# First projection of a two-layer decoder: batches that run into each other, with a second buffer for u and z

## The reference, cut to what matters

```python
x  = h * rsqrt(mean(h**2, -1) + eps) * norm_w            # 256 x 512
xz = x @ in_proj_w.T + in_proj_b                         # 512 -> 2 x 1536
x, z = xz[..., :1536], xz[..., 1536:]
xc = conv over 4 tokens of x, per feature; then u = silu(xc)
z  = silu(z)                                             # the gate
# of u: w_dt @ u and the mean over each of 24 heads (48 numbers a token)
```

## Time and profile before

| | |
|---|---|
| time, median of 3 runs | 4777.92 us (4775.51 to 4779.34) |
| the profiled execution | 4790.36 us, of it span 4788.6 us |
| TensorE / VectorE / ScalarE / GpSimd busy, whole span | 82% / 59% / 35% / 29% |
| mean granted TensorE clock, whole span | 0.914 of full speed |
| first store of u_feat issued (batch 0) | 68.92 us |
| last store of u_feat issued (batch 7) | 429.81 us |
| first instruction of the next stage's queue | 446.71 us |

### The profile page before, as it was taken

How to read it: one execution, slowest core, us unless ns; L and a number is a source line. 1 busy time by engine, 2 the same in 40 slices (tenths; PEclk the granted TensorE clock), 3 DMA queues, 4 the chain that set the end, 5 groups by cost and what they waited for, 6 DMA issues and landing times. The chain is left out here.

```text
span 4788.6 us, 61695 instructions
## 1 busy us (share of the span) xinstructions
PE 3915.2 (82%) x19902; PEld 3042.3 (64%) x19902; DVE 2804.6 (59%) x4963; ACT 1669.4 (35%) x3411; POOL 1386.2 (29%) x1202
## 2 busy tenths in 40 slices
PE   7886899989999597759995994787877689839992
PEld 7886777767777475554445873555556467627772
DVE  5554445454544476972227866999999654533335
ACT  4333322232222120042214764555555422203431
POOL 0000000000000005662225525999999500010002
PEclk9998999999999898969997997999999899959996
DMA  3323433443343452119977544222330211023324
GB/s 110 128 93 126 115 90 86 105 111 91 86 105 91 141 165 69 39 46 336 321 246 220 167 148 162 84 84 84 105 128 29 92 45 66 31 82 103 105 96 119
DMA packets 532330, 556.51 MB, mean 116 GB/s; under 512 B 157795, under 2 KB 431523, under 8 KB 526544
## 3 DMA queue, kind: packets, MB, share of 16 engines
q1 hardware_dynamic: 497728, 470.19, 32.2%
q0 software_dynamic: 29632, 75.97, 4.8%
q10 hardware_dynamic: 4816, 8.53, 0.5%
HBM read 440.09 MB, written 135.43 MB: 120 GB/s over the span
## 5 line engine op out<-in xcount | busy, mean ns | idle before, releaser
L2337 PE MATMUL d_py<-d_h,d_ident 128*128 128x256 f32 x2048 | 522.7, 412 | 177.7 <-POOL d_h L2167 155.4
L2175 POOL TENSOR_TENSOR d_dBu<-d_B,d_dtu 128x1024 f32<-128x1024 f32 x256 | 597.1, 2367 | 118.0 <-DMA d_dt<-dt 118.0
L2337 PEld LDWEIGHTS d_py<-d_h,d_ident 128*128 128x128 f32 x2048 | 412.9, 206 | 284.0 <-POOL d_h L2167 184.3
L723 PE MATMUL a_pB<-a_uhi,a_whi 128*128 128x512 f32 x1152 | 484.6, 421 | 44.2 <-DVE a_ulo L610 44.0
L723 PE MATMUL a_pB<-a_uhi,a_wlo 128*128 128x512 f32 x1152 | 455.8, 396 | 0.0
L723 PE MATMUL a_pB<-a_ulo,a_whi 128*128 128x512 f32 x1152 | 454.5, 395 | 0.0
L2221 ACT ACTIVATE d_ph<-d_dt,d_A 128x255 f32<-128x255 f32 x1024 | 425.8, 461 | 0.1
L2281 DVE TENSOR_TENSOR_SCAN d_ph<-d_ph,d_dBu 128x1024 f32<-128x1024 f32 x160 | 365.9, 2287 | 24.5 <-ACT d_ph L2221 12.1
L1058 POOL TENSOR_TENSOR b_kv<-b_c 128x128 f32 (+11 forms) x256 | 100.3, 431 | 774.1 <-DMA b_c<-ctx_turned 770.4
L530 POOL DMA_DIRECT2D a_uraw<-u_feat x48 | 25.8, 539 | 1023.9 <-DVE a_ulo L610 583.8
L723 PEld LDWEIGHTS a_pB<-a_uhi,a_whi 128*128 128x128 f32 x1152 | 218.8, 190 | 110.6 <-DVE a_wlo L614 36.6
(11 more groups left out here) (481 smaller groups left out, 9384.9 us busy)
## 6 DMA issues: line engine op xcount, KB each, us to landing
c_gu<-w_gu SPq DMA_DIRECT2D x64, 768.0 KB, 6.6
a_wraw<-w_bc SPq DMA_DIRECT2D x48, 768.0 KB, 7.5
a_alall<-alpha SPq DMA_DIRECT2D x24, 1024.0 KB, 5.2
c_wd<-w_down SPq DMA_DIRECT2D x64, 256.0 KB, 7.5
slots_y<-c_y POOLq DMA_DIRECT2D x64, 256.0 KB, 7.1
f_w1r<-w SPq DMA_DIRECT2D x64, 256.0 KB, 2.8
f_w2r<-w SPq DMA_DIRECT2D x64, 256.0 KB, 2.9
d_B<-bc SPq DMA_DIRECT2D x7, 2048.0 KB, 14.2
```

Source lines behind the costliest of these rows:

```text
L723: ins = nc.tensor.matmul(out, a[:, k, cols], b[:, k, ts], start=(k == 0 and n == 0), stop=(k == F - 1 and n == 2))
L2175: pool.tensor_tensor(dBu[c % RB][:, :, :], B_sb[i][:, q * G:(q + 1) * G, :], dtu_sb[i][:, f, :].unsqueeze(1).to_broadcast([P, G, L]), ALU. ...
L2337: ins = nc.tensor.matmul(py[f % 2][:, 0:L], ident_sb[:, :], h_sb[c % RH][:, n, :], start=False, stop=(q == Q - 1 and n == G - 1))
```

## The change: what it does

- u and z get two buffers each. The second ones lie over the 12 raw weight buffers, which are free once batch 0 has split them. xnT_hi and xnT_lo get two buffers each too.
- x of the next batch is turned inside this batch: `stats` in block 5, behind z(4) and u(4); xn on VectorE in block 7; the eight transposes behind pz(8); xnT_hi in block 9, xnT_lo in block 10.
- u's rows are turned in six portions, of 4 blocks and one half of the tokens each. Four stand in the same batch (behind pz(5), pz(6), pz(9), pz(10)), two in the next one (behind pz(1) and pz(2)); each copy by VectorE stands one block later, the last two in blocks 1 and 2 of the next batch.
- dt(0) to dt(10) stand together behind pz(11), since pT serves for turning x before that; dt(11) stands in the next batch behind pz(0). z(11) and u(11) are computed in the next batch behind xpad(0).
- Stores: z_feat ahead of dt_mean. ident and norm_w come by ScalarE's queue with a semaphore of their own, the two weights of dt have another, and TensorE starts when ident and norm_w are there.
- The hardware loop runs three times over two batches.

```diff
-    NORM_AT = 6
+    STATS_AT, NORM_AT, TURN_AT, HI_AT, LO_AT = 5, 7, 8, 9, 10
+    ROWS_AT = {5: 0, 6: 1, 9: 2, 10: 3}
+    KEPT_AT = {6: 0, 7: 1, 10: 2, 11: 3}
...
+        u_sb = [m.sb("u0", [P, F, L]), nc.alloc_sbuf_tensor_at("a1_u1", [P, F, L], F32, offset=over)]
+        z_sb = [m.sb("z0", [P, F, L]), nc.alloc_sbuf_tensor_at("a1_z1", [P, F, L], F32, offset=over + 4 * F * L)]
...
+        def reached(b, done):
+            return max(done, 0) if is_first(b) else b * F + done
+        def rows(n):
+            return n // 2, n % 2
+        def batches(eng, batch):
+            batch(0, 0, False)
+            with eng.Fori(0, NB // 2 - 1) as r:
+                for i in range(2):
+                    batch(2 * r + 1 + i, 1 - i, False)
+            batch(NB - 1, 1, True)
...
 # ScalarE
+            def batch(b, i, last):
+                for f in range(F):
+                    act.wait_ge(s_px, b * F + f + 1)
+                    act.wait_ge(s_conv, reached(b, f - 1))
+                    nc.scalar.activation(xpad[f % 2][:, 3:3 + L], px[f % 2][:, 0:L], ACT.Identity, ...).then_inc(s_xpad, 1)
...
+                    if f >= 1:
+                        gate(b, i, f - 1)
+                        value(b, i, f - 1)
+                    elif not is_first(b):
+                        gate(b - 1, 1 - i, F - 1)
+                        value(b - 1, 1 - i, F - 1)
+                    if f == STATS_AT and not last:
+                        stats(b + 1)
+                    if f == HI_AT and not last:
+                        turned(b + 1, 1 - i)
...
 # VectorE, behind conv(f)
+                    if not is_first(b):
+                        if f == 1:
+                            means(b - 1)
+                            kept(b - 1, 4)
+                        if f == 2:
+                            kept(b - 1, 5)
+                    if f in KEPT_AT:
+                        kept(b, KEPT_AT[f])
+                    if f == NORM_AT and not last:
+                        norm(b + 1, link)
+                    if f == LO_AT and not last:
+                        turned(b + 1, 1 - i)
...
 # TensorE, behind pz(f)
+                    if not is_first(b):
+                        if f == 0:
+                            dt(b - 1, 1 - i, F - 1)
+                        if f == 1:
+                            row_major(b - 1, 1 - i, 4)
+                        if f == 2:
+                            row_major(b - 1, 1 - i, 5)
+                    if f in ROWS_AT:
+                        row_major(b, i, ROWS_AT[f])
+                    if f == TURN_AT:
+                        pe.wait_ge(s_dtm, b)
+                        if not last:
+                            norm(b + 1)
                 if not last:
-                    pe.wait_ge(s_dtm, b + 1)
-                    norm(b + 1)
...
+                    pe.wait_ge(s_xnTl, b * KD + 2 * KD)
+                for k in range(F - 1):
+                    dt(b, i, k)
```

More of the change, by code:

```diff
@@ L123, in group, with is_first @@
                 split(n, *CHUNKS[n])
[L125 to L131, removed]
+        def is_first(b):
+            return isinstance(b, int) and b == 0
+        def reached(b, done):
[8 more added lines that the diff above has]
+            batch(NB - 1, 1, True)
         @block.sync
@@ L144, in load @@
                 sp.dma_start(x_sb[:, :, :], x[bass.ds(b * L, L), :].rearrange("(c p) n -> p c n", p=P)).then_inc(s_x, 16)
-            def batch(b, last, first=False):
+            def batch(b, i, last):
                 if not last:
@@ L187, in stats, with turned @@
                 assert link.count[0] == LINKS_A
-            def turned(b):
+            def turned(b, i):
                 act.wait_ge(s_T, b + 1)
                 for k in range(KD):
-                    nc.scalar.activation(xnT_hi[:, k, :], pT[:, k // 2, (k % 2) * L:(k % 2 + 1) * L], ACT.Copy,
+                    nc.scalar.activation(xnT_hi[i][:, k, :], pT[:, k // 2, (k % 2) * L:(k % 2 + 1) * L], ACT.Copy,
                                          scale=nw_sb[:, k:k + 1]).then_inc(s_xnT, 1)
[L195 to L203, removed]
-                        group(split, f + 2)
-                    if f == NORM_AT and not last:
-                        stats(b + 1)
[L207 to L228, removed]
+            def gate(b, i, g):
+                if g == 0 and not is_first(b):
+                    act.wait_ge(s_out_z, b * 16 - 16)
+                act.wait_ge(s_pz, b * F + g + 1)
+                nc.scalar.activation(z_sb[i][:, g, :], pz[g % 2][:, 0:L], ACT.Silu, bias=bz_sb[:, g:g + 1]).then_inc(s_z, 1)
@@ L230, in _ @@
+            act.wait_ge(s_set, 3)
+            stats(0)
+            group(split, 0)
+            act.wait_ge(s_turner, 32)
+            turned(0, 0)
+            group(split, 1)
+            act.wait_ge(s_const, 64)
+            batches(act, batch)
+            gate(NB - 1, 1, F - 1)
+            value(NB - 1, 1, F - 1)
         @block.vector
@@ L271, in batch @@
                     ins.then_inc(s_conv, 1)
-                    if f == NORM_AT + 1 and not last:
+                    if not is_first(b):
[7 more added lines that the diff above has]
+                    if f == NORM_AT and not last:
                         norm(b + 1, link)
+                    if f == LO_AT and not last:
+                        turned(b + 1, 1 - i)
                 assert last or link.count[0] == LINKS_V
[L275 to L291, removed]
+            norm(0)
+            group(split, 0)
+            dve.wait_ge(s_turner, 32)
+            turned(0, 0)
+            group(split, 1)
+            dve.wait_ge(s_const, 64)
+            batches(dve, batch)
+            means(NB - 1)
+            kept(NB - 1, 4)
+            kept(NB - 1, 5)
         @block.tensor
         def _(pe):
-            pe.wait_ge(s_const, 16 * CONSTS)
+            pe.wait_ge(s_turner, 32)
             def parts(out, a, a_cols, b, b_cols, k):
@@ L310, in norm, with dt @@
                 ins.then_inc(s_T, 1)
-            def batch(b, last, first=False):
-                pe.wait_ge(s_xnTl, b * KD + KD)
[L315 to L321, removed]
+            def dt(b, i, k):
+                if k == 0:
+                    pe.wait_ge(s_heads, 32)
+                pe.wait_ge(s_u, b * F + k + 1)
+                for c in range(2):
+                    ins = nc.tensor.matmul(pT[:, c, 0:H2], u_sb[i][:, k, c * P:(c + 1) * P], wdt_sb[:, k, :], start=(k == 0), stop=(k == F - 1))
+                if k == F - 1:
+                    ins.then_inc(s_dt, 1)
@@ new lines, in row_major, with batch @@
+            def row_major(b, i, n):
+                j, c = rows(n)
+                pe.wait_ge(s_u, b * F + j * 4 + 4)
+                pe.wait_ge(s_ut, max(n - 1, 0) if is_first(b) else b * 6 + n - 1)
+                for q in range(4):
+                    ins = nc.tensor.transpose(pu[n % 2][:, q * P:(q + 1) * P], u_sb[i][:, j * 4 + q, c * P:(c + 1) * P], ident_sb[:, :])
+                ins.then_inc(s_pu, 1)
+            def batch(b, i, last):
+                pe.wait_ge(s_xnTl, b * KD + KD)
+                x_parts = (xnT_hi[i], xnT_lo[i])
```

95 lines of the change are left out of this document (55 added, 40 removed).

## The result

| | before | changed |
|---|---|---|
| time, median | 4777.47 us (4775.51 to 4779.34) | 4731.92 us (4729.30 to 4736.24) |
| profiled execution | 4790.36 us | 4734.08 us |
| last store of u_feat issued | 429.81 us | 385.96 us |
| next stage's first load issued | 446.71 us | 401.83 us |

The ratio is 0.9906, 95% interval 0.9888 to 0.9923. The change takes away 45.6 us; 37.6 were forecast (4740, range 4718 to 4760). The stage itself is 44.9 us shorter in the two profiled executions. The other 11.4 us between their spans lie behind 446.71 and 401.83, where both kernels do the same work; the two medians do not show them.

A forecast was written before the change was run, and what follows sets the result against it. TensorE was taken to bound the stage, busy 45.7 of 51.57 us a batch. Clean gain 61.9 us, minus 9.6 for late x and 14.7 for the clock, left 37.6: 4777.9 to 4740 us, range 4718 to 4760.

The forecast's parts named there:

- the rival in which the clock holds: At the dt block between batches: no wait there, so the full clock stays; 52.3 us less, 4726; chance 0.24.
- TensorE's floor: TensorE's matmuls, dt loads, transposes and changes between kinds in one batch: 43.3 us.
- Clean period: One steady batch: 43.3 us of TensorE work plus 0.4, 0.2 and 0.2 for waits and semaphores, 44.1 us.
- Stats and the table load: ScalarE behind u(4): stats takes 4.4 us, xpad(6) precedes the 1.28 us silu load; the 2.0 us hole closes without slack.
- The estimate by the drain: Stats on ScalarE: a 1.38 us drain per table switch would make it some 7 us, losing about 2.8 a batch; not adopted.
- The load of x: Next x, queued behind u_tok, reaches stats 0.6 to 2.0 us late; 1.2 taken for each of six batches.
- The price added for the clock behind these waits: After stats waits for x, one wait in four lowers the clock: 0.25 x 1.75 = 0.4 us a batch.
- The clock: At the narrow dt block between batches: 4.2 us of slow clock cost 2.1 at each of seven changes, 14.7 us.
- a stretch at each: Sign in the profile: a stretch of clock near 0.50 at each change of batch.
- the 16-column row: Profile row of 64 narrow matmuls: gapless for 13.8 us at clock 0.50, so gapless work alone does not raise it.
- The start: Before batch 0's first blocks: turning at 10.4, pz(0) at 18.8 after the eighth weight chunk's split; 5.4 us gained.
- Batch 0 and the end: Batch 0 ends at 58.8, with dt block 63.8; batch 7 takes 37.5 plus 2.0 to u(11) and its store.

The follow-up runs named there:

- spread kernel: Changed kernel with x of batch b+2 loaded ahead of u_feat, x turned in pu's banks, dt among the blocks: 4729.7 us, ratio 0.9859; again 4730.7, 0.9862.
- wide one: Changed kernel with dt matmuls of 128 columns where there are as many, only the first 48 read: 4732.2 us, ratio 0.9895 to the kernel before.
- earlier x: Changed kernel with the load of x of batch b+2 issued ahead of u_feat of batch b: 4724.3 us, ratio 0.9874 to the kernel before.
- both edits: Changed kernel with x of batch b+2 loaded ahead of u_feat of batch b and dt matmuls of 128 columns: 4719.8 us, ratio 0.9871.
- closed order: Changed kernel with z(11), u(11), dt(11) and the last two portions with copies at their own batch's end: 4734.9 us, 0.9895; with 128-column dt 4726.8, 0.9853.
- old start: Changed kernel with ident and norm_w back in GpSimd's queue and TensorE's first instruction waiting for all eight constants: 4756.5 us, ratio 0.9917.

## Why the prediction was right

It was right in direction and in range, and the two losses that it priced, x and the clock, are the two that the runs found. The size of the clock term was off, and one step of the start was right in its number by luck. By the median the result is as near to the rival in which the clock holds (4726) as to the forecast (4740); by the last store of u_feat 43.9 us were gained, nearer to 37.6 than to 52.3.

- *TensorE's floor, 43.3 us.* The spread kernel runs at 43.2 to 43.6 with TensorE busy for all of it. *Clean period, 44.1*: 43.9 with both losses taken away.
- *Stats and the table load.* xpad(6) does go ahead of the load, and stats to z(5) is 4.8 us with xpad in between. The estimate by the drain that the Trainium skill gives (ScalarE: Activation LUTs, "What ACT_TABLE_LOAD costs"), 2.8 us a batch more, is refuted by this trace too: the load at 185.56 follows xpad directly, and z(5) follows the load.
- *The load of x.* Late by 0.6 to 2.0, 1.2 taken; it is 1.5, and undoing it gave back the 9.2 us that the waits add up to. The price added for the clock behind these waits, 0.4 a batch, did not come in the changed kernel. Of 24 such waits in the traces of four kernels one was followed by a slow stretch, in the wide one (137 us); one in four was taken.
- *The clock.* 2.1 a change was taken, 14.7 in all. The four stretches are 20.5 us long, at most 10.2 lost, and taking them away gave 9.2 beside the earlier x. That a block of narrow matmuls can cost the clock was right, and the size too large, since three of seven changes have no stretch; a stretch at each was also named as a sign. This term is 5.5 of the 6.3 us between 37.6 and the 43.9 by the last store. The rival by which the clock holds, since nothing waits, is false at four of seven changes: of the 16-column row and the rule of gaps that the Trainium skill gives (TensorE: Matmul & The Clock Gate, "Why this matters for your kernels"), the row was the better guide. The reading of the kernel before that stands ahead of this term is not exact: there six of seven changes had a stretch, not each (the change behind batch 0 had none, 73 to 81 us at 1.00), and three more stood inside batches, at 52, 103 and 260 us, the last two behind the 2.0 us waits of pz(7).
- *The start.* The turning starts at 10.58 (10.4 forecast) and pz(0) at 18.77 (18.8 forecast); 5.4 of gain forecast, 5.7 by the mark. But pz(0) was to wait for the split of the eighth weight chunk, with px(0) done long before. In the trace that split is done at 18.39, and pz(0) follows px(0), which starts at 16.04 instead of 15.2 and takes 2.7 us instead of 1.43. Two errors met in one number, and that it fits is luck. Why these twelve matmuls take so long was not found; the view by stretches has the clock at 1.00 there.
- *Batch 0 and the end.* With its dt block batch 0 was to end at 63.8 and u_feat to follow 3.1 later, 66.9; it was 67.6. The last store clean at 367.9; it was 367.6 with both edits.
- *What the prediction did not see*: that the running over, which it priced only through its effects, is what makes x late, and that it gives next to nothing with dt in one block. It named u_tok as waiting for copies in blocks 1 and 2, but did not ask what the closed order would have cost.

## What to carry to other kernels

When a batch boundary is filled, ask which part fills it: here a block of independent work (dt) covers the wait for the last u, and letting batches overlap on top of it gave 0.5 us at most and delayed the copies that gate a store, and with it a load queued behind the store. A load that could be issued early should not stand in a queue behind a store that waits for computed data. And moving many short matmuls into one block keeps TensorE's records gapless and can still cost its clock: spread them among wide ones, or give them more columns where the weight load sets the pace anyway.

## What the runs showed of the hardware

- A float32 matmul with its weight load of 128 columns takes the same time with 48 and with 128 moving columns, 5.11 and 5.15 us for 44 (40 of them with 128, four with 96).
- The granted clock fell to 1.2 GHz in or behind a block of 44 to 48 such matmuls with 48 columns, without a wait ahead of it: at 4 of 7 changes of batch in two executions of the changed kernel, at 3 with the earlier x, at 3 with the old start, at 7 of 7 where the block had 48 and eight transposes behind it. It never fell there with 128 columns (28 changes in four kernels), nor in the spread kernel, where the same matmuls stood in groups of four or eight among those of 256 columns (two executions).
- The changed kernel lies 18 us apart in two groups of runs (4731.9 and 4749.7), and the kernel before as much (4777.5 and 4795.7), so only kernels of one group compare by their time.
